# A two-block diffusion transformer on one core: row statistics of x and of the last context on ScalarE instead of VectorE

## What is computed

```python
h = ln(x) * (1 + sc_msa) + sh_msa            # n1
x = x + self_attn(h) * g_msa                 # w: windows of 128, rolled by 64, 16 heads of 16
h = ln(x) * (1 + sc_mca) + sh_mca            # n2
x = x + topk_cross_attn(h, ctx) * g_mca      # t: softmax over the 16 largest of 256 scores
h = ln(x) * (1 + sc_mlp) + sh_mlp            # n3
x = x + swiglu(h) * g_mlp                    # m: 256 -> 2 x 1024 -> 256
# second block: adaptive norm of x (n4) and of the same ctx (nc), plain cross attention l
x = x + cross_attn(ada_ln(x), ada_ln(ctx))
```

## Time and profile before

| | us |
|---|---|
| median of 3 runs | 1279.81 (1276.47 to 1280.52) |
| profiled execution, time | 1284.55 |
| profiled execution, span | 1282.4 |
| mean granted TensorE clock | 0.978 |

### The profile page before, as it was taken

How to read it: one execution, slowest core, us unless ns; L and a number is a source line. 1 busy time by engine, 2 the same in 40 slices (tenths; PEclk the granted TensorE clock), 3 DMA queues, 4 the chain that set the end, 5 groups by cost and what they waited for, 6 DMA issues and landing times. The chain is left out here.

```text
span 1282.4 us, 39016 instructions
## 1 busy us (share of the span) xinstructions
PE 1200.6 (94%) x13666; PEld 853.9 (67%) x13666; DVE 1128.0 (88%) x3812; ACT 1034.6 (81%) x2193; POOL 855.0 (67%) x1134
## 2 busy tenths in 40 slices
PE   6778899999999999999999999999999999989987
PEld 6665566667676776767676766767676776656654
DVE  3579999899999999999999989999999999997443
ACT  3745688889898979889797979889797979786764
POOL 1415597959587877859686877959596867776210
PEclk8988999999999999999999999999999999999989
DMA  7542021202121121212021212212121111111111
GB/s 200 149 92 56 22 60 35 63 25 57 39 56 44 47 64 52 57 34 69 21 68 35 64 47 54 58 31 57 28 59 42 47 48 35 43 26 27 26 26 34
DMA packets 111391, 67.25 MB, mean 52 GB/s; under 512 B 13836, under 2 KB 107870, under 8 KB 111198
## 3 DMA queue, kind: packets, MB, share of 16 engines
q1 hardware_dynamic: 109166, 63.71, 19.0%
q10 hardware_dynamic: 2032, 1.05, 0.5%
HBM read 22.33 MB, written 4.19 MB: 21 GB/s over the span
## 5 line engine op out<-in xcount | busy, mean ns | idle before, releaser
L1246 ACT ACTIVATE prob<-turned_score 128x1024 f32<-128x1024 f32 x320 | 325.8, 1018 | 78.5 <-PE turned_score L908 76.1
L1521 POOL TENSOR_TENSOR pair<-full,pair 128x512 f16<-128x512 f32 x182 | 210.9, 1162 | 118.2 <-ACT pair L1201 113.6
L1405 DVE MATCH_REPLACE8 rest<-top,score 128x256 f32<-128x256 f32 x512 | 208.9, 417 | 0.0
L1419 DVE MATCH_REPLACE8 far<-best,rest 128x256 bf16<-128x256 f32 x512 | 206.4, 412 | 0.0
L1402 DVE MAX8 top<-score 128x8 f32<-128x256 f32 x512 | 193.9, 421 | 13.2 <-PE score L908 12.4
L1527 POOL TENSOR_SCALAR far<-far 128x512 bf16<-128x512 bf16 x256 | 158.6, 620 | 41.4 <-DVE far L1419 20.9
L1392 DVE TENSOR_REDUCE rowmax_l<-score 128x4 f32<-128x1024 f32 x121 | 147.8, 1221 | 30.4 <-PE score L908 24.3
L908 PE MATMUL work<-pair_n,w_m_hi 128*128 128x256 f16 x1024 | 173.5, 273 | 0.3 <-ACT full L1194 0.2
L908 PE MATMUL work<-pair_n,w_m_lo 128*128 128x256 f16 x512 | 139.6, 273 | 0.0
L1201 ACT ACTIVATE pair<-full 128x512 f16<-128x512 f32 x192 | 121.1, 631 | 20.2 <-DMA k_stack_l<-pair 1.8
L908 PEld LDWEIGHTS work<-pair_n,w_m_hi 128*128 128x128 f16 x1024 | 96.1, 98 | 19.1 <-issue 7.6
(11 more groups left out here) (212 smaller groups left out, 3206.8 us busy)
## 6 DMA issues: line engine op xcount, KB each, us to landing
k_stack_t<-pair SPq DMA_DIRECT2D x96, 64.0 KB, 2.5
k_stack_l<-pair SPq DMA_DIRECT2D x96, 64.0 KB, 2.6
q_stack_w<-pair SPq DMA_DIRECT2D x93, 64.0 KB, 2.6
k_stack_w<-pair SPq DMA_DIRECT2D x93, 64.0 KB, 2.6
q_stack_t<-pair SPq DMA_DIRECT2D x93, 64.0 KB, 2.6
q_stack_l<-pair SPq DMA_DIRECT2D x93, 64.0 KB, 2.6
ctx_t<-in_ctx_turned SPq DMA_DIRECT2D x16, 256.0 KB, 2.9
ctx_l<-in_ctx SPq DMA_DIRECT2D x16, 256.0 KB, 3.1
```

What stands on the lines that cost most here:

```text
L1246: act.activation(prob[:, at:at + 2, :], both_b[:, :, :], ACT.Exp).then_inc(exp_done, 1)
L1405: m = dve.match_replace(rest[p % 2][:, t, :], eight[:, t, :], bank[:, t * L:(t + 1) * L], -FAR)
L1419: m = dve.match_replace(far[p % NFAR][:, t, :], best[p % 2][:, t, :], rest[p % 2][:, t, :], -FAR)
L1521: pool.tensor_tensor(pr[:, 1, :, :], whole[:, :, :], pr[:, 0, :, :], ALU.subtract).then_inc(split_lo, 1)
```

## The change

The statistics of n1 and nc for batches 1 to 15 are taken in the way in which those of n2, n3 and n4 are. A new ScalarE step `sm` copies each of the two 128x256 tiles of x (or of ctx) into a full tile and sums the rows as it does; `ms` on GpSimd makes minus the mean of it; `sq` on ScalarE sums the squares of the difference; `rs` goes on from there. The `bn` steps of batches 1 to 15 leave VectorE's order. Batch 0 stays as it was. All five orders and `IDLE_WORK` are laid out anew: ScalarE's has 60 steps more (30 `sm`, 30 `sq`), GpSimd's 30 more (`ms`), VectorE's 30 fewer; TensorE's and SyncE's hold the same steps in another order. `sm` and `sq` of n1 and nc take full tiles too.

```diff
+def summed(s, b):
+    return s in ("n2", "n3", "n4") or b > 0
...
-IDLE_WORK = ("pj_wq:0:0=59 gd_w:0:0=30 gd_w:0:1=21 gd_w:0:2=11 bk_w:0:0=17 x4_n2:0:0=25 pj_tq:0:0=38 a_w:1:0=13 "
-             "a_t:0:0=16 a_w:1:2=35 o_w:1:0=14 gd_t:0:1=27 b_t:0:3=7 gd_t:0:2=9 o_t:0:2=11 a_t:1:0=11 pr_w:2:0=12 "
-             "a_l:13:7=10 ot_l:13:0=8 xt_m:15:0=6 x4_n4:15:0=5 a_l:15:1=15 a_l:15:3=11 a_l:15:7=16 bk_l:15:0=14 "
+IDLE_WORK = ("pj_wq:0:0=59 a_w:0:0=21 gd_w:0:0=31 gd_w:0:2=10 bk_w:0:0=17 xt_w:0:0=16 x4_n2:0:0=25 pj_tq:0:0=38 "
+             "a_t:0:0=20 a_w:1:2=44 a_w:1:3=6 a_t:0:1=13 pj_wq:2:0=14 gd_t:0:1=7 b_t:0:2=12 pr_w:1:0=14 "
+             "x4_n2:1:0=43 pr_w:2:0=12 bk_t:15:0=9 ot_l:13:0=10 x4_n4:15:0=10 pj_lq:15:0=28 bk_l:15:0=14 "
              "pr_l:15:0=33")
...
         full_no = {k: n + 1 for n, k in enumerate(
-            [k for k in plan["act"] if k[0][:2] in ("sp", "fo", "sq") and k[0] != "sp_cx"])}
+            [k for k in plan["act"] if k[0][:2] in ("sp", "fo", "sq", "sm") and k[0] != "sp_cx"])}
...
+        def means_before(s, b):
+            return b if s in ("n2", "n3", "n4") else b - 1
...
+                elif kind == "sm":
+                    if s == "n1":
+                        act.wait_ge(x_in[b % NX], 48 * (b // NX + 1))
+                    else:
+                        act.wait_ge(ctx_in["l"], 16 * (b + 1))
+                    if b > 1:
+                        act.wait_ge(mean_done[s], means_before(s, b))
                     n = full_no[piece, b, 0] - 1
                     if n >= NFULL:
                         act.wait_ge(*full_freed(full_keys[n - NFULL]))
+                    src, copied = ctx_tile["l"] if s == "nc" else X[b % NX], full_tile(piece, b)
                     for t in range(LT):
+                        m = act.activation(copied[:, t, :], src[:, t, :], ACT.Copy, accum_out=row_sum[s][:, t:t + 1])
+                    m.then_inc(full_done, 1)
+                elif kind == "sq":
+                    act.wait_ge(mean_done[s], means_before(s, b) + 1)
...
                 if kind == "ms":
-                    pool.wait_ge(x_added[ADDED[s]], b + 1)
+                    if s in ADDED:
+                        pool.wait_ge(x_added[ADDED[s]], b + 1)
+                    else:
+                        pool.wait_ge(full_done, full_no["sm_" + s, b, 0])
                     pool.tensor_scalar(rstd[s][:, 2, :], row_sum[s][:, :], -1.0 / C, 0.0, ALU.mult,
                                        ALU.add).then_inc(mean_done[s], 1)
```

More of the change, by code:

```diff
@@ L563, in build @@
         LN = ("n1", "n2", "n3", "n4", "nc")
-        SUMMED = ("n2", "n3", "n4")
-        stats = {s: sb(f"stats_{s}", [P, LT, 6], F32) for s in LN if s not in SUMMED}
-        mv = {s: sb(f"mean_var_{s}", [P, LT, 2], F32) for s in LN if s not in SUMMED}
-        row_sum = {s: sb(f"row_sum_{s}", [P, LT], F32) for s in SUMMED}
-        square_sum = {s: sb(f"square_sum_{s}", [P, LT], F32) for s in SUMMED}
+        stats = {s: sb(f"stats_{s}", [P, LT, 6], F32) for s in ("n1", "nc")}
+        mv = {s: sb(f"mean_var_{s}", [P, LT, 2], F32) for s in ("n1", "nc")}
+        row_sum = {s: sb(f"row_sum_{s}", [P, LT], F32) for s in LN}
+        square_sum = {s: sb(f"square_sum_{s}", [P, LT], F32) for s in LN}
         rstd = {s: sb(f"rstd_{s}", [P, 3, LT], F32) for s in LN}
@@ L668, in build @@
         guard_out = {s: sem(f"guard_out_{s}") for s in "wtl"}
-        stat_done = {s: sem(f"stat_{s}") for s in LN if s not in SUMMED}
-        mean_done = {s: sem(f"mean_{s}") for s in SUMMED}
+        stat_done = {s: sem(f"stat_{s}") for s in ("n1", "nc")}
+        mean_done = {s: sem(f"mean_{s}") for s in LN}
         norm_done = {s: sem(f"norm_{s}") for s in LN}
@@ L800, in full_freed @@
                 return low_done(s, key[1])
-            if kind == "sq":
+            if kind in ("sq", "sm"):
                 return full_done, full_no[key]
@@ L1201, in _ @@
                     act.activation(pair_tile(s, b)[:, 0, :, :], tile[:, :, :], ACT.Copy).then_inc(split_hi, 1)
-                elif kind == "sq":
-                    act.wait_ge(mean_done[s], b + 1)
+                elif kind == "sm":
[5 more added lines that the diff above has]
+                        act.wait_ge(mean_done[s], means_before(s, b))
                     n = full_no[piece, b, 0] - 1
@@ L1206, in _ @@
                         act.wait_ge(*full_freed(full_keys[n - NFULL]))
-                    squares = full_tile(piece, b)
+                    src, copied = ctx_tile["l"] if s == "nc" else X[b % NX], full_tile(piece, b)
                     for t in range(LT):
-                        m = act.activation(squares[:, t, :], X[b % NX][:, t, :], ACT.Square, bias=rstd[s][:, 2, t:t + 1],
+                        m = act.activation(copied[:, t, :], src[:, t, :], ACT.Copy, accum_out=row_sum[s][:, t:t + 1])
+                    m.then_inc(full_done, 1)
+                elif kind == "sq":
+                    act.wait_ge(mean_done[s], means_before(s, b) + 1)
+                    n = full_no[piece, b, 0] - 1
+                    if n >= NFULL:
+                        act.wait_ge(*full_freed(full_keys[n - NFULL]))
+                    src, squares = ctx_tile["l"] if s == "nc" else X[b % NX], full_tile(piece, b)
+                    for t in range(LT):
+                        m = act.activation(squares[:, t, :], src[:, t, :], ACT.Square, bias=rstd[s][:, 2, t:t + 1],
                                            accum_out=square_sum[s][:, t:t + 1])
@@ L1493, in _ @@
                     n = rs_no[piece, b, 0] - 1
-                    if s in SUMMED:
+                    if summed(s, b):
                         pool.wait_ge(full_done, full_no["sq_" + s, b, 0])
```

## The result

The changed kernel takes 1299.19 us (median of 4 runs, 1293.43 to 1304.72) beside 1278.14 us for the kernel before (4 runs, 1275.87 to 1280.52). The ratio is 1.0156, 95% interval 1.0126 to 1.0186: about 20 us slower, where 1275.4 us and 0.34% faster was forecast. The prediction missed, and the time lies above its range.

A forecast was written before the change was run, and what follows sets the result against it. TensorE was taken to bound 320 to 1040 us, VectorE 80 to 240. Terms +0.5, -2.9, -1 and -1 sum to -4.4 us, span 1282.4 to 1278.0, median 1275.4 us; range 1265 to 1289.

The forecast's parts named there:

- moved work: All five orders laid out anew, 913 of 1639 TensorE steps changing rank; costed at nothing beyond +0.5 us in the first 80 us.
- VectorE's relief: 28.8 us of statistics leave VectorE; gains 2.9 us from 80 to 240, up to 5.6 from 320 to 1040, 1 elsewhere.
- ScalarE's added work: 60 sm and sq steps of 0.99 us, 39.6 us in the steady part; loss taken as 4.6 us, bound 10.4.
- in the width of the range, not a case of its own: A cover opening up somewhere in the new orders was left to the forecast's range, with no separate chance.
- The ring of full tiles: Splits may wait for GpSimd's subtraction on shared tiles; costed at nothing, or 1 to 2 us at each of 11 places.
- The start: First 80 us: packed ScalarE work against an earlier GpSimd step; between -1 and +2 us, taken as +0.5.
- the sign named for this term: First top-16 search beginning over 2 us later or earlier than before would show the start term wrong.
- ScalarE as the bound: Steady part: exponentials queue behind sm and sq, so TensorE waits; +9.5 us, 1289 us, chance 0.24.
- Its sign: From 320 to 1040 us, turned_score's wait for prob over 20 us and TensorE's share below 97.5% would confirm the ScalarE rival.
- The rival by the Trainium skill's rule: VectorE is the bound all along, so all 28.8 us come back: 1251 us, chance 0.05.

The follow-up runs named there:

- Experiment 1: Kernel before, old orders, with VectorE's n1 and nc statistics for batches 1 to 15 left out and nothing in their place: 1281.16 us, ratio 1.0007.
- 6: Old orders without those statistics, plus 120 unused ScalarE copies and squares with sums, in pairs where VectorE's statistics stood, nobody waiting for them: 1304.37 us, ratio 1.0205.
- 9: Old orders without those statistics, the same unused ScalarE work placed one instruction at a time before the eight instructions with ScalarE's longest idle gaps: 1288.26 us, ratio 1.0069.
- 2: Changed kernel, new orders, with sm, sq and ms of n1 and nc taken out and no VectorE statistics either: 1295.39 us, ratio 1.0132 to the kernel before.
- 4: Two kernels without either kind of statistics, switching orders after the first 250 us: new then old 1.0053, old then new 1.0086, to the kernel before.
- 11: Changed kernel with its new orders, but copies and squares of x and ctx go to one spare tile outside the ring: 1296.43 us, ratio 1.0136.
- 5: Kernel before with old orders, statistics moved to ScalarE where VectorE's stood, written to a spare tile outside the ring: 1304.96 us, ratio 1.0199.

## Why the prediction was wrong

The right reading was that TensorE has the least room. The step that failed is the one on moved work, which put the re-laid orders at nothing; they cost 1.25 points, 16 us. The gain of 9.5 us expected from VectorE's relief did not come either. In the order of the experiments the terms are 0.07 points (relief), 1.25 (orders) and 0.24 (ScalarE's work), together the 1.56 measured. Term by term:

- **VectorE's relief** (2.9 us from 80 to 240, up to 5.6 in the steady part, 1 for the rest): worth nothing. Experiment 1 is this term alone, 1.0007. I let TensorE's waits for VectorE shrink in the ratio of VectorE's idle times. They did not: the three rows were 15.9 us before and are 15.1 in 1 (7.9, 3.6 and 3.6), where 10.3 was expected. I now take such a wait of 0.3 us for the way from an operand to the next step and not for a lack of VectorE time; no run tests that by itself. And in 80 to 240 us a VectorE at 98% did not set the pace alone either: in 1 the search went from 1.0 us behind at batch 0 to 0.5 us ahead at batch 4, where 2.9 were counted, and the runs show nothing of it.
- **ScalarE's added work** (4.6 us taken, 10.4 as the bound): some 3 us in the new orders, near the 4.6 taken, but 24 us in the old ones. I costed it against ScalarE's idle time, 84.7 us for 39.6 of work, and thought the work free as long as that covers it. It isn't in the old orders, where ScalarE had 84.5 us idle in 1 for the same work: what counts is the slack ahead of each result that TensorE comes for, 0.5 us at the place shown in 6. The idle time lies in gaps at other places, and 9 shows what filling those costs: 9 us in place of 26. My figure for ScalarE's load was a tenth too high (0.89 us a step in place of 0.99); the rule for its price was wrong, and that its result came near is luck.
- **Moved work** (nothing): the costliest error. The new orders are 1.25% slower than the old ones for the same work (experiments 1 and 2), in the steady part about 1 us in every batch (4). I had counted that 913 of 1639 TensorE steps change rank and looked for what each of them passes only in the first 80 us; "in the width of the range, not a case of its own" was the step that failed. In return these orders hold ScalarE's work for some 3 us, where the old ones pay 24, and in them the whole move is a gain (1.0228 to 1.0156).
- **The ring of full tiles** (nothing): at run time 0 to 3 us, so nearly right. But by my reading of the lists it is what rules the old orders out, and I didn't see that I was pricing two changes tied together.

**The start** was sized +0.5, bounds -1 to +2. The first top-16 search began at 80.2 us (78.4 before), 1.8 later, at a granted clock of 0.80 over the first 80 us in place of 0.87, so the sign named for this term came out inside its 2 us. By batch 2 the lag is 6.9 us. How much of that is ScalarE's packed start is not shown: two executions with the same lists up to 250 us differ by 4.2 us at that search (4), and with the same ScalarE work outside the ring it began 0.7 us late (11).

**The rivals.** The one that ends slower, ScalarE as the bound, has the right mechanism for the old orders (5, 6), at 24 us where I had a net 9.5, but not for the changed kernel, where ScalarE's work adds 3 us. Its sign was to be a wait for prob over 20 us and TensorE under 97.5%; TensorE has 97.3% (700.28 of 720) and the wait 12.0 us. The sign was ill chosen as well: in 6, where nothing but ScalarE's time is at work, the same row reads 16.0 us, as the rest goes into other waits. The rival by the Trainium skill's rule (Perfetto Trace Analysis, Identifying the Most-Contended Engine), that the weight loads' 69.6% leave TensorE headroom and VectorE is the engine to relieve, is refuted here by 1: the statistics steps off VectorE, 28.8 us by their starts, brought nothing. (That page names the share of peak arithmetic beside the weight loads' share; it was not worked out here.)

**Still open** is why the new orders lose 1 us a batch. From 1 to 2 TensorE's idle time from 320 to 1040 us goes from 12.5 to 21.6 us, by small amounts: 2.8 us more ahead of the w branch's scores, 1.5 ahead of the transposes of normed tiles, 1.4 ahead of w's guards, 1.3 ahead of w's attended, 1.2 ahead of gd_t (worked out from both traces). Of the 2.8 us, 1.7 is a single wait for the copy into the stack k_stack_w, which SyncE issues: SyncE's order, in which steps of batches 5 to 12 lie up to 22 places off, is a suspect as much as the others, and I tested none of them alone but GpSimd's. In these batches most steps keep their place or move by up to 3 on TensorE and GpSimd, single ones by up to 14 and 13. And whether some other layout holds ScalarE's work without loss was not tried. It could win little: taking away VectorE's statistics alone (1.0007) or ScalarE's second powers alone (0.9998) gives nothing in the old orders; both at once was not tried. No version here beats the kernel before.

## What to carry to other kernels

Where TensorE is at 98% and every engine follows a list laid out ahead, as here, don't price added work by an engine's idle time or a relief by its busy time: look at the slack between each result and the step that comes for it, and reckon with a knee such as this kernel has on ScalarE, with nothing gained below the present load and a loss at once above it. A change that comes with re-laid orders is two changes, and the orders are priced by running them without the moved work. Try added work one instruction at a time in the gaps in which the engine waits, not where the work that it replaces stood on another engine; here that cut the price by two thirds, for work that nobody waits for.

## What the runs showed that was not expected

The same 78 us of ScalarE instructions (the sum of their durations) cost 26 us in one layout and 9 in another. Relief of either engine beside TensorE gave nothing that the runs can tell, 28.8 us off VectorE (1.0007) or 21 us off ScalarE in the steady part (0.9998), but half of the move's work onto ScalarE cost 1.2%. And one engine's list taken from another layout, in batches 5 to 12 only 8 of its 376 steps off by more than six places, cost 79 us (1.0619).
